# Row maxima of attention scores from the high parts alone, two heads at a time in 64-row tiles of TensorE

## The reference

```python
q = einsum('bsm,hmd->bhsd', x, wq); k = ...; v = ...
scores = einsum('bhsd,bhtd->bhst', q, k) * scale
out = einsum('bhst,bhtd->bhsd', softmax(scores), v)   # then the output projection
```

## Time and profile before

| | us |
|---|---|
| median of 3 runs | 3798.69 |
| runs | 3795.74, 3799.52, 3798.69 |
| the profiled execution | 3801.34 |
| its span | 3799.5 |
| TensorE busy | 3605.6 (95%) |
| GpSimd busy | 2625.3 (69%) |
| VectorE busy | 2240.1 (59%) |
| ScalarE busy | 1671.8 (44%) |
| exponentials of attention a | from 106.1 to 1710.7 |
| exponentials of attention b | from 2056.6 to 3566.1 |

### The profile page before, as it was taken

The page is one execution under the profiler, slowest core; times in us unless marked ns, Lnnn a source line. Parts: engine busy times, 40 slices in busy tenths (PEclk is TensorE's granted clock), DMA queues, the critical chain, the costliest instruction groups (busy, mean ns, idle before and its releaser), DMA issues. The chain is left out here.

```text
span 3799.5 us, 61436 instructions
## 1 busy us (share of the span) xinstructions
PE 3605.6 (95%) x17248; PEld 2331.5 (61%) x17248; DVE 2240.1 (59%) x2976; ACT 1671.8 (44%) x3216; POOL 2625.3 (69%) x1467
## 2 busy tenths in 40 slices
PE   3999999999999999997985999999999999999799
PEld 2566666666666666656873565655565556665488
DVE  4444444444444444435766777777777777777354
ACT  2444444444444444444543444444444444444354
POOL 2687778777777787773323787888788878887521
PEclk9999999999999999998997999999999999999899
DMA  6433443344334433411115444444444454444100
GB/s 200 94 76 81 111 89 76 78 111 87 77 81 105 90 78 85 89 40 33 45 56 105 83 87 103 85 86 86 102 85 86 86 104 86 86 86 79 40 18 28
DMA packets 423700, 313.74 MB, mean 83 GB/s; under 512 B 258848, under 2 KB 296608, under 8 KB 422560
## 3 DMA queue, kind: packets, MB, share of 16 engines
q1 hardware_dynamic: 415616, 286.78, 36.0%
q10 hardware_dynamic: 7968, 25.69, 2.1%
HBM read 88.35 MB, written 21.50 MB: 29 GB/s over the span
## 5 line engine op out<-in xcount | busy, mean ns | idle before, releaser
L926 POOL TENSOR_TENSOR a_rs<-a_rs,a_p 128x1024 f32<-128x1024 f32 x384 | 917.0, 2388 | 339.2 <-ACT a_p L831 321.7
L851 DVE TENSOR_REDUCE a_nmax<-a_ps_x 128x1 fp32r<-128x1024 f32 x508 | 622.3, 1225 | 777.7 <-PE a_ps_x L631 774.0
L926 POOL TENSOR_TENSOR b_rs<-b_rs,b_p 128x1024 f32<-128x1024 f32 x384 | 916.9, 2388 | 234.9 <-ACT b_p L831 214.8
L851 DVE TENSOR_REDUCE b_nmax<-b_ps_x 128x1 fp32r<-128x1024 f32 x508 | 621.9, 1224 | 298.2 <-PE b_ps_x L631 293.8
L831 ACT ACTIVATE a_p<-a_ps_s 128x512 f32<-128x512 f32 x1024 | 530.0, 607 | 421.4 <-PE a_ps_s L647 421.1
L831 ACT ACTIVATE b_p<-b_ps_s 128x512 f32<-128x512 f32 x1024 | 530.1, 609 | 342.7 <-PE b_ps_s L647 342.2
L663 PE MATMUL b_ps_o<-b_p,b_v 128*64 128x512 f32 x2048 | 467.7, 598 | 0.0
L663 PE MATMUL a_ps_o<-a_p,a_v 128*64 128x512 f32 x2048 | 467.7, 598 | 0.0
L646 PE MATMUL b_ps_s<-b_q,b_k 128*128 128x512 f32 x1024 | 418.3, 409 | 3.7 <-ACT b_p L831 2.1
L646 PE MATMUL a_ps_s<-a_q,a_k 128*128 128x512 f32 x1024 | 416.3, 406 | 2.4 <-DMA a_q<-a_nmax 1.5
L647 PE MATMUL a_ps_s<-a_q,a_k 128*128 128x512 f32 x1024 | 403.3, 394 | 0.0
(11 more groups left out here) (171 smaller groups left out, 5603.2 us busy)
## 6 DMA issues: line engine op xcount, KB each, us to landing
a_q<-a_nat_h SPq DMA_DIRECT2D x250, 128.0 KB, 2.4
a_k<-a_nat_h SPq DMA_DIRECT2D x250, 128.0 KB, 2.4
b_q<-b_nat_h SPq DMA_DIRECT2D x250, 128.0 KB, 3.3
b_k<-b_nat_h SPq DMA_DIRECT2D x250, 128.0 KB, 3.3
a_rinv<-rows_a SPq DMA_DIRECT2D x128, 128.0 KB, 2.9
b_rinv<-rows_b SPq DMA_DIRECT2D x128, 128.0 KB, 3.4
a_q<-a_nat_l SPq DMA_DIRECT2D x125, 128.0 KB, 2.4
a_k<-a_nat_l SPq DMA_DIRECT2D x125, 128.0 KB, 2.4
```

Of the source, the lines that this page charges most:

```text
L851: dve.reduce_max(nmax[:, g % 2, head, qi:qi + 1], max_banks(t, c)[:, 0:2, :].rearrange("p a b -> p (a b)"), AX_X, negate=True).then_inc(s_ ...
L926: pool.tensor_tensor(out, out, p[:, bb, i, :], ALU.add).then_inc(s_sum, 1)
```

## The change

Each maxima step now takes one half of the keys and both heads, in place of one head and all keys. It makes two matmuls of 64 rows: head 0 from partitions 0 to 63 of `q1` and `k1`, head 1 from partitions 64 to 127 of `q1` and `k2`. Both are q_high times k_high. They stand in two tiles of 64 rows by 128 columns of the array, and write to the two banks of `ps_x`. The count of maxima matmuls, of their columns and of their weight loads stays. VectorE's reduction of a step gives two numbers per row in place of one, over the same 1024 columns, into the new tile `half_max`. A smaller-of-two operation (of negated maxima) joins the halves into `nmax`: one after step 5 for three query tiles, one after step 7 for the fourth. The semaphore `s_red` counts 10 per group in place of 8, and SyncE's waits before `shift` follow that.

```diff
+        half_max = sb("half_max", [P, 2, 2, BT])
...
+        def reduced(c):
+
+            return 10 * (c // 8) + c % 8 + (2 if c % 8 > 5 else 1)
+
         def maxima(pe, t, c):
 
-            g, qi, head = c // 8, (c % 8) // 2, c % 2
+            g, qi, half = c // 8, (c % 8) // 2, c % 2
...
-            pe.wait_ge(s_red, due(t, 32, c - 1 if first_group(t, c) else c))
-            for half in range(2):
-                mm = pe.matmul(max_banks(t, c)[:, half, :], q1[:, slot, head, qi * P:(qi + 1) * P],
-                               k1[:, pair % 2, head, half * BLOCK:(half + 1) * BLOCK], start=True, stop=True)
+            pe.wait_ge(s_red, due(t, 40, reduced(c - 2 if first_group(t, c) else c - 1)))
+            for head, keys in ((0, k1), (1, k2)):
+                rows = slice(D * head, D * (head + 1))
+                mm = pe.matmul(max_banks(t, c)[:, head, :], q1[rows, slot, head, qi * P:(qi + 1) * P],
+                               keys[rows, pair % 2, head, half * BLOCK:(half + 1) * BLOCK], start=True, stop=True)
             mm.then_inc(s_m, 1)
...
         def reduce(dve, t, c):
-            g, qi, head = c // 8, (c % 8) // 2, c % 2
+            g, qi, half = c // 8, (c % 8) // 2, c % 2
             dve.wait_ge(s_m, due(t, 32, c + 1))
-            if c % 8 == 0:
+            dve.reduce_max(half_max[:, half, :, qi], max_banks(t, c)[:, 0:2, :], AX_X, negate=True).then_inc(s_red, 1)
+            if c % 8 == 5:
                 dve.wait_ge(s_shift, due(t, 512, 128 * (g - 1)))
-            dve.reduce_max(nmax[:, g % 2, head, qi:qi + 1], max_banks(t, c)[:, 0:2, :].rearrange("p a b -> p (a b)"), AX_X,
-                           negate=True).then_inc(s_red, 1)
+                row_max(dve, t, c, slice(0, BT - 1))
+            if c % 8 == 7:
+                row_max(dve, t, c, slice(BT - 1, BT))
+
+        def row_max(dve, t, c, cols):
+            dve.wait_ge(s_red, due(t, 40, reduced(c)))
+            dve.tensor_tensor(nmax[:, (c // 8) % 2, :, cols], half_max[:, 0, :, cols], half_max[:, 1, :, cols],
+                              ALU.min).then_inc(s_red, 1)
...
-                sp.wait_ge(s_red, due(t, 32, 8 * (u + 2) - 2))
+                sp.wait_ge(s_red, due(t, 40, 10 * (u + 2) - 3))
                 for qi in range(BT - 1):
                     shift(sp, u + 1, qi)
-                sp.wait_ge(s_red, due(t, 32, 8 * (u + 2)))
+                sp.wait_ge(s_red, due(t, 40, 10 * (u + 2)))
```

More of the change, by code:

```diff
@@ L625, in maxima @@
                 if g % 2 == 0:
-                    for half in range(2):
-                        pe.wait_ge(s_stack[1 + half], due(t, 2 * SD, SD * (pair + 1)))
+                    for n in (1, 2):
+                        pe.wait_ge(s_stack[n], due(t, 2 * SD, SD * (pair + 1)))
                 pe.wait_ge(s_stack[3 * (g % 2)], due(t, 2 * SD, SD * (pair + 1)))
-            pe.wait_ge(s_red, due(t, 32, c - 1 if first_group(t, c) else c))
-            for half in range(2):
-                mm = pe.matmul(max_banks(t, c)[:, half, :], q1[:, slot, head, qi * P:(qi + 1) * P],
-                               k1[:, pair % 2, head, half * BLOCK:(half + 1) * BLOCK], start=True, stop=True)
+            pe.wait_ge(s_red, due(t, 40, reduced(c - 2 if first_group(t, c) else c - 1)))
[3 more added lines that the diff above has]
+                               keys[rows, pair % 2, head, half * BLOCK:(half + 1) * BLOCK], start=True, stop=True)
             mm.then_inc(s_m, 1)
```

## The result

The changed kernel takes 3989.09 us, the median of 4 runs from 3988.34 to 3991.20; the kernel before took 3799.11 us beside it. The ratio is 1.0503, with a 95% interval from 1.0490 to 1.0515: 190 us slower. I had forecast 3885 us. The sign was right, and of the loss I had less than half. By attention (from its first matmul to its last) the change costs 64 us in a and 124 us in b.

What follows compares the result with a forecast made beforehand. TensorE was taken to bound both attentions. Tiling changes net of paired matmuls +97 us, joins nothing, 10 us given back: +87 on 3801.3 is 3888, the median 2.6 lower, so 3885 us; range 3715 to 4010 us.

Steps and rivals of the forecast that it cites:

- What bounds the kernel: Both attentions: TensorE, busy 1496.7 and 1455.4 of 1500 us, at a granted clock of 1.00 and 0.98.
- The two matmuls of a step run together: Maxima steps: the two 64-row matmuls take 0.235 us together, saving 0.235 us a step.
- Rival 4: Maxima steps: the two matmuls run in turn and the tiling still changes, 4126 us; chance 0.05.
- A change of tiling costs 0.41 us where both sides are full-array: Maxima step between full-array neighbours: pays 0.41 us, saves 0.235, so 0.17 us dearer; +97 us over 128 groups.
- Rivals 1 and 2: Maxima steps: row tiles change no tiling, 3590 us, chance 0.13; only gap or load paid, 3725 us, chance 0.12.
- Given back: Attention b: TensorE's waits for VectorE shrink as steps lengthen, between 0 and 40 us, taken as 10.
- X: Tiling-change cost of a maxima step between full-array neighbours: 0.41 us, forecast from 0.35 to 0.48, break-even 0.29.
- The joins cost nothing: VectorE: two joins a group at 164 ns each, 0.33 us a group, costed at nothing.
- without cover: VectorE's joins if no other work hid them: 128 x 0.33 = 42 us.
- Cover: Attention b: VectorE busy 896 of 1200 us, a reduction has 8 matmuls of scores beside it, so joins cost nothing.
- The slack of a shift: Last shift of a group: lands 1.0 us before the scores need it, against 0.17 us of join.
- Rival 3: Maxima steps: the two loads run in turn, 0.11 us more a step, +113 us, about 3998 us; chance 0.09.

Runs made afterwards that it cites:

- e5: Kernel before with 64-row tiles, no join, only in the three maxima steps of a group beside values or row sums: 3791.36 us, ratio 0.9971.
- e6: Kernel before with 64-row tiles, no join, only in the five maxima steps of a group between full-array work: 3877.53 us, ratio 1.0203.
- e1: Kernel before with 64-row tiles in all maxima steps, both tiles for one head, so no join: 3867.96 us, ratio 1.0179.
- e2: Changed kernel with 128-row maxima matmuls again, split keys and two-input joins kept: 3976.94 us, ratio 1.0465.
- e4: Changed kernel with 128-row maxima matmuls and the join as a reduction over one tile: 3821.25 us, ratio 1.0053.
- e3: Changed kernel, 64-row tiles kept, with the join as a reduction over one tile holding both halves: 3874.39 us, ratio 1.0194.

## Why the prediction was wrong

- **What bounds the kernel**: right. TensorE, at the full granted clock; all that changed the time did so by TensorE's work or its waits.
- **The two matmuls of a step run together**: right; 0.50 us for the two. Rival 4 is out.
- **A change of tiling costs 0.41 us where both sides are full-array**: right in kind and nearly in size. A step between full-array neighbours became 0.157 us dearer in attention a where I had 0.17 (0.165 ahead of a projection, 0.144 behind an output projection); load, pair and gap together take 0.43 us where my terms make 0.44. One with tiled work on a side became 0.04 cheaper, where I had 0.03. The counts hold as well: 380 of the 1024 steps stand beside tiled work. Rivals 1 and 2 are out; e5 and e6 show both signs separately.
- **Given back**: I took 10 us. e1 gives 43 x 2 - 68, about 18.
- So this part of the sum, 97 - 10 = 87 us, measured 68 us (e1). Two small slips of the sum changed nothing: unrounded, X = 0.41 gives 100 us and not 97, and X from 0.35 to 0.48 gives 3839 to 3948 us and not 3835 to 3940. And no matmul is missing from the earlier trace rows: the 8 that bring 1016 to 1024 write to `ps_s`, in the first group.
- **The joins cost nothing: this is the step that failed.** I priced a join at 164 ns from the earlier trace rows. That row is from the first 100 us, where GpSimd has little to do; I carried it to a place where GpSimd is busy 957 of 1200 us. There a join takes about 1.0 us. I called 42 us the cost "without cover"; e2 puts joins and split keys at 177 us, 156 of them for the second input (e4), and beside the tiles the second input is worth 190 - 75 = 115 us (the change against e3).
- **Cover**: I read VectorE's share of 75% as room. Its order matters more: the add that TensorE's projection of v waits for, the shifts and the next reduction all stand behind a join. The slack of a shift, 1.0 us against 0.17, was read in attention a and for a join of 0.16 us; against one of up to 2.0 us in b it is gone. Even with short joins e4 shows 21 us where I had none.
- **Rival 3** (the loads of a step run in turn) gave 3998 us, near the time measured, for a cause that isn't there: the two loads take 0.19 us together. A time that fits a rival doesn't speak for its mechanism. By luck, too, 3989 us lies inside my range of 3715 to 4010: the range reached so far only to take in this rival, and no case to which I gave a chance had the joins cost anything.

The Trainium skill, page "SBUF — State Buffer", section "SBUF: two separate sides", says that VectorE and GpSimd share a pair of ports under an exclusive lock, which VectorE takes for an operation with two inputs in SBUF when GpSimd's instruction reads SBUF, and that the later one is held for the whole instruction of the other. The traces here agree: GpSimd's sums read `rs` and `p` in SBUF, the join with two inputs ends 18 to 28 ns after the one that is running, and the join with one input never takes more than 168 ns. I hadn't weighed that rule in the prediction. Nearly every operation of VectorE in the attentions of before reads PSUM or one tile, so the rows that I took from there show no such wait.

The trace of before does show it, in the feed-forward networks, outside the rows that I read. L380 is a TENSOR_TENSOR with both inputs in SBUF, 128 times in all with a median of 692 ns. The timeline from 3613.5 to 3616:

```profile
3611.91 3.40 POOL L437 TENSOR_TENSOR x<-x,f_b2s 128x1024 f32<-128x1024 f32 x1 [1.97 <-DVE f_h L108]
...
3613.49 2.37 DVE L380 TENSOR_TENSOR f_gl<-f_g,f_gh 128x512 fp32r<-128x512 f32 x1 [0.46 <-ACT f_gh L351]
```

Nine of the 128 begin like this well inside an L437 and take 0.98 to 2.37 us; each ends some 0.55 us after it. So the price of a two-input operation beside GpSimd could be read before the change was made. Not each L380 that overlaps an L437 is held: those that begin just ahead of it, or right behind another L380, take 0.69 us as ever. L437 is the longer for them: 2.34 us with none, up to 2.79 with one, 3.40 with two and 3.98 with three. There GpSimd is the one that waits.

## What to carry to other kernels

Before adding even a tiny VectorE operation to a stage where GpSimd is busy, count its inputs in SBUF: with two it can take as long as what is left of GpSimd's running instruction, here 1.0 us on average instead of 0.16, and all that is behind it in VectorE's order is late by that. Tiles that halve the rows pay only next to work that is tiled already: here a step of two matmuls wins about 0.25 us (an estimate from the 0.41 paid and the 0.157 lost), and some 0.2 us are paid for each side at which the tiling changes, so steps of 0.5 us scattered among full-array work lose. Price an operation from a row of the stage in which it will run, not from the cheapest row of its kind.

## What the runs showed that I had not expected

- A VectorE operation of 2 to 6 numbers per row took up to 2.0 us, depending on what GpSimd was running (162 ns at least, 1094 and 1428 ns the medians of attention a and b).
- Splitting GpSimd's sums, which is more work for it (2 x 1283 ns in place of 2378), took 54 us off the loss, since it shortens what others wait for.
- The costs of the two parts, 68 and 177 us, are together 190 us.
